# A two-layer kernel on one core: the last two expert tiles added by selection products, K and V weights split among the tiles, the barrier between the layers taken out

## The chip, the cores and the metric

The kernel runs on one core of a Trainium2 chip. The core has a matmul engine (PE, with its weight loads as PEld), a vector engine (DVE), an activation engine (ACT), a general engine (POOL) and a queue engine (SP, in the trace SPq) that issues most transfers. Each works through its own instructions in order and waits on semaphores for the others. The metric is the time of the kernel on the device in microseconds (us); lower is better.

## What is computed

Two layers on 2 x 512 tokens of 256 numbers, in fp32. The first layer runs a state-space scan beside a mixture of experts (each token goes to 2 of 8 experts), multiplies the two and adds the result to the tokens; the second does the same with attention and a sign-weight layer.

```python
x = L0_attn_x
xn = _layernorm(x, axis=-1)
s = _L0_attn_ref(xn, ...)              # projections, convolution, chunked scan, out projection
g = _silu(_L0_ffn_ref(xn, ...))        # top-2 of 8 experts, weighted sum of their outputs
x = x + s * g
xn = _layernorm(x, axis=-1)
s = _L1_attn_ref(xn, ...)              # 32 query heads, 8 key/value heads of 64
g = _silu(_L1_ffn_ref(xn, ...))
x = x + s * g
```

## The kernel before, in words

**Experts.** The 2 x 1024 (token, expert) pairs are sorted by expert into NJ = 23 tiles of 128 rows. For a tile j, POOL gathers the tokens' rows from memory (X on POOL), PE transposes them (X, turn_x), and multiplies with the expert's weights in three pieces (H1, H2, H3 in hidden); ACT takes the silu and DVE multiplies the halves to hE; PE projects back (P, project). DVE scales each row by its weight into y_row (rows, P on DVE), and POOL scatters the 128 rows to y_rows in memory, at the place given by to_row (P on POOL). The weights of a tile lie in one of three slots of wm; SP loads them as slots come free. X and P of PE share one PSUM bank: turn_x(j) waits for row_taken of tile j - 3.

**Scan.** The 1024 tokens are also cut into 8 chunks of 128. Chunk c has on PE the steps F (scan_decay: two fp32 matmuls of 512 columns), C (scan_front: a 128x128 product and four transposes), Y (scan_back) and O (out_rows). Between them ACT does exps (F) and scales (C), DVE the products (C, Y), y_lo (L) and the residual (O, which adds to semaphore s_part), POOL the mixes.

**Order.** The function side_by_side gives each step of tiles and chunks a place on one axis, 4 units for a tile, and each engine does its own steps in that order. CHUNK_AT says where each chunk begins. In the steps' names below the number is the tile or the chunk: P20 is the projection of tile 20, Y7 the scan_back of chunk 7.

**Between the layers.** After the last tile SP waits until all scatters have landed (row_out) and reads y_rows back as gy, two rows for each token. DVE adds the two (mixed_pair), ACT takes the silu, DVE multiplies with the scan's result s_tok and adds to x_tok (add_pair) and makes row statistics (pair_stats), for 4 pairs of token tiles. SP then loads the K and V weights of the second layer (kv_raw), ACT scales and rounds them to the upper part (kv_hi), POOL takes the rest (kv_lo). Then every engine calls end_phase, a barrier of all five. After it come the last statistics, the normalisation (xn1), its transposes (turn_norm), the K, Q and V products (make_k, make_q, make_v) and the attention proper.

```python
def end_phase(eng):
    k = ends[eng.engine] = ends.get(eng.engine, 0) + 1
    eng.drain().then_inc(phase_done, 1)
    eng.wait_ge(phase_done, 5 * k)
```

Of the kernel before, what the change touches and what calls it, by code (L numbers as in the profile page):

```python
# [152 lines left out]
K_MOVES = 4 * 16  # L153


def layered_kernel(nc, x, params, consts, select, rope, w_in, w_out, w_moe, w_moe_tail, w_qkv, w_o, w_sign, out):
# [4 lines left out]
    with ctx:  # L161
# [103 lines left out]
        w_out_sb = Map(weights_at)("w_out_sb", [P, NCH, C])  # L265
# [50 lines left out]
        assert back.at <= last.at
        kv_raw = last("kv_raw", [P, 2, KC, KVH * HD])
        kv_hi = last("kv_hi", [P, 2, KC, KVH * HD], F32R)
        kv_lo = last("kv_lo", [P, 2, KC, KVH * HD], F32R)
# [19 lines left out]
        q_mix = kv_raw[:, :, :, :]  # L339
# [12 lines left out]
        p_hi = kv_hi[:, :, :, :].rearrange("p a k n -> p (a k) n")  # L352
        p_lo = kv_lo[:, :, :, :].rearrange("p a k n -> p (a k) n")
# [24 lines left out]
        phase_done = sem("phase_done")  # L378
# [50 lines left out]
        ends = {}  # L429

        def end_phase(eng):

            k = ends[eng.engine] = ends.get(eng.engine, 0) + 1
            eng.drain().then_inc(phase_done, 1)
            eng.wait_ge(phase_done, 5 * k)

# [23 lines left out]
        def _(sp):  # L460
# [6 lines left out]
            sp.dma_start(w_out_sb[:, :, :], w_out).then_inc(w_out_in, 16)  # L467

# [166 lines left out]
        def _(dve):  # L635
# [47 lines left out]
            vec.memset(ssm[:, :, 0:TAPS - 1], 0.0).then_inc(ones_ready, 1)  # L683
            then(vec.memset(chosen[:, NT, :], 0.0))
# [213 lines left out]

            for engine, op, n in side_by_side():
# [31 lines left out]
            def mixed_pair(n):  # L931
                dve.wait_ge(pair_in[n], 32)
                ts = slice(2 * n, 2 * n + 2)
                TT(gate_y[:, ts, :], gy[:, 0, ts, :], gy[:, 1, ts, :], ALU.add).then_inc(mixed, 1)
# [150 lines left out]
        def _(act):  # L1085
# [39 lines left out]
            for n, (b, kind, m) in enumerate(PROJS):  # L1125
# [49 lines left out]
            for engine, op, n in side_by_side():  # L1175
# [39 lines left out]
            for n in range(NT // 2):
                act.wait_ge(mixed, n + 1)
                actv(gate_y[:, 2 * n:2 * n + 2, :], gate_y[:, 2 * n:2 * n + 2, :], ACT.Silu).then_inc(gated, 1)
            actv(sv[:, 8, :], sv[:, 0, :], ACT.Sqrt)
            act.wait_ge(kv_in, 96)
            actv(kv_raw[:, 0, :, 0:2 * P], kv_raw[:, 0, :, 0:2 * P], ACT.Copy, scale=HD ** -0.5).then_inc(k_scaled, 1)  # L1220
            actv(kv_hi[:, 1, :, :], kv_raw[:, 1, :, :], ACT.Copy)
            act.wait_ge(k_scaled, 1)
            actv(kv_hi[:, 0, :, 0:2 * P], kv_raw[:, 0, :, 0:2 * P], ACT.Copy).then_inc(w_hi_done, 1)
            end_phase(act)


# [121 lines left out]
        def _(gp_):  # L1348
# [53 lines left out]
            for engine, op, n in side_by_side():  # L1402
# [14 lines left out]
            gp_.wait_ge(w_hi_done, 3)  # L1417
            GT(kv_lo[:, 1, :, :], kv_raw[:, 1, :, :], kv_hi[:, 1, :, :].bitcast(F32), ALU.subtract)
            GT(kv_lo[:, 0, :, 0:2 * P], kv_raw[:, 0, :, 0:2 * P], kv_hi[:, 0, :, 0:2 * P].bitcast(F32), ALU.subtract).then_inc(w_lo_done, 1)
            end_phase(gp_)  # L1420


# [62 lines left out]
        def _(pe):  # L1485
# [231 lines left out]
            def make_k(r, b, k, bk):  # L1717
                w_h, w_l = (wk_hi, wk_lo) if r else (kv_hi[:, 0, :, :], kv_lo[:, 0, :, :])
                on_rows(bk[:, :], lambda c: w_h[:, c, k * P:(k + 1) * P], lambda c: w_l[:, c, k * P:(k + 1) * P], b).then_inc(kx_full, 1)

            def make_v(t):
# [3 lines left out]
                for c in range(KC):  # L1725
                    ins = split3(bank[t // TB * 2 + t % 2][:, :], xnT_hi[:, c, ts], xnT_lo[:, c, ts], kv_hi[:, 1, c, :], kv_lo[:, 1, c, :],
# [198 lines left out]
```

## Time and profile before

| what | value |
|---|---|
| time, median of 3 runs | 783.19 us (781.56 to 783.24) |
| the profiled execution | 780.78 us, of which the span of instructions is 779.0 us |
| busy in the span | PE 706.5 us (91%), DVE 477.7 (61%), ACT 417.9 (54%), POOL 399.3 (51%) |
| chain that ended last | PE 64%, DVE 10%, POOL 9%, ACT 8%, issue 6% |

The profile is of one execution, 2.4 us below the median of the three timed ones. A share of busy time is an average over stages with different limits, so it says little of one stage. "Issue" in the chain is time in which the engine waited for nothing that the profile shows, and PEclk or clock is the granted clock of PE as a part of full speed. PE's instructions in fp32 are recorded twice each (x16 are 8 matmuls).

### The profile page before, as it was taken

Reading aid. Unit: us, or ns where it says so; the run is one execution under the profiler, and the core shown is the slowest. Engines: PE = TensorE matmul, PEld = TensorE weight load, DVE = VectorE, ACT = ScalarE, POOL = GpSimd, SP = SyncE. Lnnn points to the kernel's source line nnn. Section 1 sums busy time; section 2 is a strip of 40 time slices with the busy share of each in tenths; the row PEclk is TensorE's granted clock in tenths of the full one; section 3 lists DMA queues with packets and bytes.
Section 4 is the critical chain, followed back from the end, with each engine's and each line's share of the span. In section 5 each row is a group of like instructions: output and inputs, shape, how many; then the busy total and the mean of one; then the engine's idle time right before and its main releaser. Section 6 shows DMA issues by size and latency. Waiting matters only on the chain.

```text
span 779.0 us, 13360 instructions
## 1 busy us (share of the span) xinstructions
PE 706.5 (91%) x4536; PEld 618.6 (79%) x4536; DVE 477.7 (61%) x1023; ACT 417.9 (54%) x1043; POOL 399.3 (51%) x451
## 2 busy tenths in 40 slices
PE   2999999999999991388889999999999999999995
PEld 2887989989989981266678888888888888888874
DVE  7582644423323445485566787777877778777764
ACT  4446244233233234236467776677766777667663
POOL 1412442332332220326777776787767877677460
PEclk9899999999999996599899999999999999999999
DMA  5075877778787505235224323322233222232001
GB/s 187 28 253 186 280 251 249 237 253 254 248 254 250 171 15 155 41 116 147 82 69 117 67 62 69 89 69 64 65 69 89 71 58 67 58 89 56 1 1 54
DMA packets 101859, 96.21 MB, mean 124 GB/s; under 512 B 50592, under 2 KB 72032, under 8 KB 101664
## 3 DMA queue, kind: packets, MB, share of 16 engines
q1 hardware_dynamic: 99584, 89.33, 39.6%
q0 software_dynamic: 2208, 6.03, 2.2%
q8 instruction: 36, 0.59, 0.3%
q14 instruction: 31, 0.25, 0.1%
HBM read 69.24 MB, written 9.31 MB: 101 GB/s over the span
## 4 chain that ended last, share of the span: by engine, by line
PE 64%; DVE 10%; POOL 9%; ACT 8%; issue 6%; SPq 1%; POOLq 1%; DMA 1%; DVEq 0%; ACTq 0%
PE bank L1631 15%; PE bank L1491 8%; PE bank L1665 8%; PE bank L1492 8%; PE bank L1493 8%; PE bank L1487 6%; POOL prob L1449 5%; ACT prob L1264 3%; PE bank L1752 3%; DVE nmax L1010 2%; PE bank L1753 2%; POOL q_lo L1461 2%; ACT kv_hi L1271 2%; DVE o_lo L1023 1%; POOL wq_lo L1429 1%
## 5 line engine op out<-in xcount | busy, mean ns | idle before, releaser
L1449 POOL TENSOR_TENSOR prob<-prob,rinv 128x128 f32<-128x128 f32 (+3 forms) x256 | 177.6, 724 | 102.1 <-DVE rinv L1015 102.1
L1264 ACT ACTIVATE prob<-bank,nmax 128x512 f32<-128x512 f32 (+3 forms) x256 | 133.2, 528 | 45.4 <-DVE nmax L1010 43.9
L1019 DVE TENSOR_TENSOR kv_lo<-bank,kv_hi 128x512 fp32r<-128x512 f32 x160 | 110.0, 687 | 52.7 <-ACT kv_hi L1271 51.8
L1271 ACT ACTIVATE kv_hi<-bank 128x512 fp32r<-128x512 f32 x160 | 96.3, 602 | 78.7 <-PE bank L1487 78.6
L1631 PEld LDWEIGHTS bank<-xgT,wm 128*128 128x128 f32 x920 | 108.1, 192 | 5.3 <-issue 3.8
L1631 PE MATMUL bank<-xgT,wm 128*128 128x128 f32 x920 | 110.3, 275 | 0.5 <-ACT xgT L1173 0.5
L1487 PE MATMUL bank<-cst,prob 128*128 128x128 f32 x640 | 97.8, 276 | 3.0 <-POOL prob L1449 1.2
L1010 DVE TENSOR_REDUCE nmax<-bank 128x1 f32<-128x512 f32 (+2 forms) x192 | 91.1, 502 | 10.8 <-PE bank L1755 10.2
L1491 PE MATMUL bank<-kv_hi,v_lo 128*128 128x128 f32 (+3 forms) x256 | 93.2, 364 | 0.3 <-DVE kv_lo L1019 0.3
L1752 PE MATMUL bank<-kT,qT 128*128 128x512 f32 (+3 forms) x256 | 81.6, 324 | 11.2 <-ACT prob L1264 7.2
L912 DVE TENSOR_TENSOR hE<-sil,bank 128x512 f32<-128x512 f32 x23 | 15.8, 688 | 111.0 <-PE bank L1631 80.5
L1493 PE MATMUL bank<-kv_hi,v_hi 128*128 128x128 f32 (+3 forms) x256 | 82.6, 323 | 0.0
L1492 PE MATMUL bank<-kv_lo,v_hi 128*128 128x128 f32 (+3 forms) x256 | 82.6, 322 | 0.0
L1415 POOL DMA_INDIRECT y_rows<-y_row,to_row x23 | 25.8, 1123 | 107.8 <-DVE y_row L885 107.8
L1487 PEld LDWEIGHTS bank<-cst,prob 128*128 128x128 f32 x640 | 73.6, 142 | 5.9 <-POOL prob L1449 3.3
L1753 PE MATMUL bank<-kT,qT 128*128 128x512 f32 (+3 forms) x256 | 74.4, 322 | 0.0
L1752 PEld LDWEIGHTS bank<-kT,qT 128*128 128x128 f32 x256 | 48.1, 188 | 20.9 <-issue 7.1
L1665 PE MATMUL bank<-wm,hE 128*128 128x256 f32 x230 | 53.5, 379 | 0.0
L1264 ACT ACTIVATION_READ_ACCUMULATOR prob<-bank,nmax 128x1 f32 x256 | 52.5, 205 | 0.0
L1753 PEld LDWEIGHTS bank<-kT,qT 128*128 128x128 f32 x256 | 48.3, 189 | 3.9
L1493 PEld LDWEIGHTS bank<-kv_hi,v_hi 128*128 128x128 f32 x256 | 48.6, 190 | 2.8
L1491 PEld LDWEIGHTS bank<-kv_hi,v_lo 128*128 128x128 f32 x256 | 48.7, 190 | 0.9 <-DVE kv_lo L1019 0.8
(301 smaller groups left out, 1479.0 us busy)
## 6 DMA issues: line engine op xcount, KB each, us to landing
wm<-in_w_moe SPq DMA_DIRECT2D x23, 1280.0 KB
wm<-in_w_moe SPq DMA_DIRECT2D x23, 640.0 KB, 5.7
qT<-q_hi SPq DMA_DIRECT2D x124, 64.0 KB, 2.0
qT<-q_lo SPq DMA_DIRECT2D x124, 64.0 KB, 2.0
k_exp<-k_rows SPq DMA_DIRECT2D x56, 64.0 KB, 2.0
wtl<-in_w_moe_tail SPq DMA_DIRECT2D x46, 64.0 KB
gy<-y_rows SPq DMA_DIRECT2D x8, 256.0 KB, 4.8
wq_raw<-in_w_qkv SPq DMA_DIRECT2D x32, 64.0 KB, 2.5
```

Source lines behind the costliest of these rows:

```text
L1019: TT(p_lo[:, b_, :], bank[2 + b_ % 2][:, :], p_hi[:, b_, :].bitcast(F32), ALU.subtract).then_inc(plo_done, 1)
L1264: ins = actv(prob[:, i % 2, h, POFF[j]:POFF[j] + (j + 1) * P], bk[:, at:at + (j + 1) * P], ACT.Exp, bias=nmax[:, i % 2, h, j:j + 1], accum ...
L1271: actv(p_hi[:, b_, :], bank[2 + b_ % 2][:, :], ACT.Copy).then_inc(phi_done, 1)
L1449: ins = GT(seg, seg, rinv[:, i % 2, k, j:j + 1].to_broadcast([P, (j + 1) * P]), ALU.mult)
L1487: return nc.tensor.transpose(dst, src, ident)
L1491: mm(dst, w_l, m_h, start=start, stop=False)
L1492: mm(dst, w_h, m_l, start=False, stop=False)
L1493: return mm(dst, w_h, m_h, start=False, stop=stop)
L1631: ins = mm(dst, w(c), xgT[:, u, c, :], start=c == 0, stop=c == KC - 1)
L1665: ins = mm(bank[3][:, 0:C], hE[:, u, i * P:(i + 1) * P], wm[:, s, i, PJ:WM] if i < FULL else ptl[:, s, :], start=i == 0, stop=i == HC - 1)
L1752: mm(dst, qs, kT[:, b, 0, 0:n], start=(h, j, at) == SCORES[k][0], stop=False)
L1753: mm(dst, qs, kT[:, b, 1, 0:n], start=False, stop=False)
```

## The change

**Tiles 21 and 22 are not scattered.** POOL has no P step for them (PICKED = 2). DVE makes for each a 128 x 8 x 128 matrix of zeros and ones (pick) that says which token each row belongs to. After the last tile PE makes for each of the 4 pairs of token tiles one sum in a PSUM bank (sum_pair): the two rows read back, each times the unit matrix, and the rows of y_row of both tiles times their selection matrices. ACT takes the silu from the bank. So that rows which no tile wrote are zero, SP fills the first 2048 rows of y_rows with zeros at the start (a memset of zeros by DVE, one transfer of 2 MB), and the first gather and the gates wait for it.

**Read-back.** SP reads back after the scatters of the first 21 tiles, once s_part is 4, into the first halves of xs and gate, which the scan has then done with.

**K and V weights.** SP loads them when row_full is 21, into the slot that tile 20 has left; ACT's rounding is the step "kv" of side_by_side at 4 * NJ - 4.6, POOL's the step at 4 * NJ - 3.7. q_mix, p_hi and p_lo get places of their own.

**Order.** CHUNK_AT goes in steps of 11.5 instead of 12.

**Barrier.** end_phase is gone from all engines; single waits stand in its place (SP for s_part = 8, POOL for row_full = 23, PE for turns_ready and w_lo_done). The transposes of the rotation tables (turns) lie between the second and third sum, and ACT's Sqrt table load ahead of the last wait.

```diff
         if j > 0:
-            z += [(at + 3.1, "PE", "P", j - 1), (at + 3.2, "DVE", "P", j - 1), (at + 3.3, "POOL", "P", j - 1)]
+            z += [(at + 3.1, "PE", "P", j - 1), (at + 3.2, "DVE", "P", j - 1)]
+        if 0 < j <= NJ - PICKED:
+            z += [(at + 3.3, "POOL", "P", j - 1)]
...
+    z += [(4 * NJ - 4.6, "ACT", "kv", 0), (4 * NJ - 3.7, "POOL", "kv", 0)] + [(42.6 + 6 * i, "DVE", "pick", i) for i in range(PICKED)]
...
-CHUNK_AT = [3 + 12 * c for c in range(NT)]
+PICKED = 2
+CHUNK_AT = [3 + 11.5 * c for c in range(NT)]
...
+            sp.wait_ge(ones_ready, 3)
+            sp.dma_start(y_rows[0:2 * T, :].rearrange("(a p) c -> p a c", p=P),
+                         zeros.unsqueeze(1).to_broadcast([P, 2 * T // P, C])).then_inc(xn_out, 16)
...
-            sp.wait_ge(row_full, NJ)
+            sp.wait_ge(row_full, NJ - 2)
+            for c in range(KC):
+                for h in range(2):
+                    load_wk(0, c, h, wk0[:, c, h * P:(h + 1) * P])
+                sp.dma_start(wv0[:, c, :].rearrange("p (g d) -> p g d", d=HD),
+                             w_qkv[:, :, c, (GQ + 1) * HD:(GQ + 2) * HD].rearrange("g p d -> p g d")).then_inc(kv_in, 16)
             yv = y_rows[0:2 * T, :].rearrange("(k t p) c -> p k t c", k=2, p=P)
             for u in range(2):
-                sp.wait_ge(row_out[u], (NJ + 1 - u) // 2 * 16)
+                sp.wait_ge(row_out[u], (NJ - PICKED + 1 - u) // 2 * 16)
+            sp.wait_ge(s_part, TB)
             for n in range(NT // 2):
                 for k in range(2):
-                    sp.dma_start(gy[:, k, 2 * n:2 * n + 2, :], yv[:, k, 2 * n:2 * n + 2, :]).then_inc(pair_in[n], 16)
...
-            end_phase(sp)
+                    sp.dma_start(gy(k, n).rearrange("p (t c) -> p t c", c=C), yv[:, k, 2 * n:2 * n + 2, :]).then_inc(pair_in[n], 16)
+            sp.wait_ge(s_part, NT)
...
+            def pick(i):
+
+                j = NJ - PICKED + i
+                then(TS(spare_f[:, 0:NT], edges[:, 0:NT], -1.0, tab[:, 1, j:j + 1], ALU.mult, ALU.add))
+                TT(picks[:, i, :, :], lane_no.unsqueeze(1).to_broadcast([P, NT, P]),
+                   spare_f[:, 0:NT].unsqueeze(2).to_broadcast([P, NT, P]), ALU.is_equal).then_inc(table_ready, 1)
...
+                elif op == "kv":
+                    act.wait_ge(kv_in, 96)
+                    actv(wk0[:, :, :], wk0[:, :, :], ACT.Copy, scale=HD ** -0.5).then_inc(k_scaled, 1)
+                    actv(wv0_hi[:, :, :], wv0[:, :, :], ACT.Copy)
+                    act.wait_ge(k_scaled, 1)
+                    actv(wk0_hi[:, :, :], wk0[:, :, :], ACT.Copy).then_inc(w_hi_done, 1)
...
+            def sum_pair(n):
+
+                dst = bank[MIXED_IN[n]]
+                pe.wait_ge(pair_in[n], 32)
+                for k in range(2):
+                    mm(dst[:, :], ident, gy(k, n), start=k == 0, stop=False)
+                for i in range(PICKED):
+                    j = NJ - PICKED + i
+                    pe.wait_ge(table_ready, 5 + i)
+                    pe.wait_ge(row_taken, j + 1)
+                    for t in range(2):
+                        ins = mm(dst[:, t * C:(t + 1) * C], picks[:, i, 2 * n + t, :], y_row[:, j % 2, :],
+                                 start=False, stop=i == PICKED - 1 and t == 1)
+                ins.then_inc(mixed, 1)
+
+            pe.wait_ge(s_part, NT)
+            sum_pair(0)
+            sum_pair(1)
             pe.wait_ge(rp4_ready, 3)
```

ACT, before, from the silu of H1 of tile 22 (sil of 128x512) to the first work after the tiles; dx are the scales of chunk 7, y_hi is ahead of O7:

```order
L1192 ACTIVATE sil<-bank 128x512
L1165 ACTIVATE dx<-xs,par 128x128 x4
L1197 ACTIVATE sil<-bank 128x128
L1198 ACTIVATE sil<-bank 64x128
L1145 ACTIVATE y_hi<-gate 128x512
L1211 ACTIVATE turns<-bank 128x512 x3
```

ACT, after, from the second half of tile 21's silu on; wk_118 is wk0 and wv_hi is wv0_hi:

```order
L1213 ACTIVATE sil<-bank 128x128
L1214 ACTIVATE sil<-bank 64x128
L1200 ACTIVATE wk_118<-wk_118 128x512
L1201 ACTIVATE wv_hi<-wv_119 128x1024
L1203 ACTIVATE wk_hi<-wk_118 128x512
L1208 ACTIVATE sil<-bank 128x512
L1213 ACTIVATE sil<-bank 128x128
L1214 ACTIVATE sil<-bank 64x128
L1155 ACTIVATE y_hi<-gate 128x512
L1227 ACTIVATE xs<-bank 128x512 x2
```

The three roundings of the K and V weights now stand between the silus of tile 21 and those of tile 22, and y_hi of chunk 7 behind both.

PE, before, from P20 (wm,hE and ptl,hE) to P21; xgT,wm x8 and x12 are H1 and parts of H2 and H3 of tile 22, decay_in is F7, CT,BT and xs are C7:

```order
L1665 MATMUL bank<-wm,hE 128x256 x5
L1665 MATMUL bank<-ptl,hE 128x256
L1572 MATMUL bank<-decay_in,cst 128x512
L1573 MATMUL bank<-decay_in,ones 128x512
L1631 MATMUL bank<-xgT,wm 128x128 x8
L1580 MATMUL bank<-CT,BT 128x128
L1487 MATMUL bank<-cst,xs 128x128 x4
L1631 MATMUL bank<-xgT,wm 128x128 x12
L1631 MATMUL bank<-xgT,wtl 128x128 x2
L1665 MATMUL bank<-wm,hE 128x256 x5
L1665 MATMUL bank<-ptl,hE 128x256
L1597 MATMUL bank<-mix,x_dt 128x128
```

PE, after, from F7 to the H1 and H2 of tile 22 that stand together behind P20; cst,xg is X of tile 22:

```order
L1581 MATMUL bank<-decay_in,cst 128x512
L1582 MATMUL bank<-decay_in,ones 128x512
L1496 MATMUL bank<-cst,xg 128x128 x2
L1640 MATMUL bank<-xgT,wm 128x128 x8
L1589 MATMUL bank<-CT,BT 128x128
L1496 MATMUL bank<-cst,xs 128x128 x4
L1640 MATMUL bank<-xgT,wm 128x128 x4
L1640 MATMUL bank<-xgT,wtl 128x128 x2
L1674 MATMUL bank<-wm,hE 128x256 x5
L1674 MATMUL bank<-ptl,hE 128x256
L1640 MATMUL bank<-xgT,wm 128x128 x16
```

F7 and C7 have moved ahead of P20, into tile 21.

DVE, before, around chunk 6's front (cbm to x_end); the y_row rows are those of tiles 17 and 18:

```order
L885 TENSOR_SCALAR y_row<-bank,tab 128x256
L912 TENSOR_TENSOR hE<-sil,bank 128x512
L843 TENSOR_TENSOR cbm<-bank,cst 128x128
L848 TENSOR_TENSOR w_end<-dts,within 128x4
L851 TENSOR_TENSOR x_dt<-bank,dts 128x512
L852 TENSOR_TENSOR x_end<-bank,w_end 128x512
L915 TENSOR_TENSOR hE<-sil,bank 128x128
L916 TENSOR_TENSOR hE<-sil,bank 64x128
L885 TENSOR_SCALAR y_row<-bank,tab 128x256
```

DVE, after, the same place; the y_row rows are those of tiles 16 and 17:

```order
L897 TENSOR_SCALAR y_row<-bank,tab 128x256
L931 TENSOR_TENSOR hE<-sil,bank 128x512
L934 TENSOR_TENSOR hE<-sil,bank 128x128
L935 TENSOR_TENSOR hE<-sil,bank 64x128
L855 TENSOR_TENSOR cbm<-bank,cst 128x128
L860 TENSOR_TENSOR w_end<-dts,within 128x4
L863 TENSOR_TENSOR x_dt<-bank,dts 128x512
L864 TENSOR_TENSOR x_end<-bank,w_end 128x512
L897 TENSOR_SCALAR y_row<-bank,tab 128x256
```

The rows of tile 17 (the second y_row) now stand behind the front of chunk 6, where before the front stood behind them.

## Rows read from the trace of the kernel before

**Rows 1.** Stages: length, busy us (count) by engine, clock, DMA share, GB/s.
```profile
100.00:284.00 184.00, 184.00 (x1330) 168.53 (x1329) 68.15 (x148) 65.18 (x138) 57.85 (x53) 1.00 0.72 230
...
293.00:324.00 31.00, 3.44 (x29) 3.23 (x30) 15.21 (x42) 8.89 (x15) 6.64 (x7) 0.60 0.47 117
```

**Rows 2.** Waits from 284 to 330 us: total, times, longest, in us.
```profile
PE bank L1487 <- DVE xn L963: 27.1, 2, 26.9
```

**Rows 3.** The chain of work: start, us, engine and line.
```profile
274.64 2.59 PE bank L1665 x12
277.23 0.86 PE bank L1572 x2
...
278.95 1.78 PE bank L1631 x16
...
311.54 7.45 POOLq L434
```

**Rows 4.** Timeline, DVE after the barrier: start, us, operation, [idle before].
```profile
319.02 0.75 DVE L946 BATCH_NORM_STATS2 stats<-x_tok 128x6 f32<-128x256 f32 x2 [7.57 <-POOLq L434]
```

**Rows 5.** Timeline, last tiles, PE, ACT and DVE.
```profile
277.07 1.02 PE L1572 MATMUL bank<-decay_in,cst 128*128 128x512 f32 x2
...
280.09 1.28 ACT L1192 ACT_TABLE_LOAD   x1
...
280.57 0.39 PE L1580 MATMUL bank<-CT,BT 128*128 128x128 f32 x2
...
281.23 2.84 PE L1631 MATMUL bank<-xgT,wm 128*128 128x128 f32 x24
...
281.88 1.26 ACT L1165 ACTIVATE dx<-xs,par 128x128 f32<-128x128 f32 x4
...
287.06 0.46 PE L1597 MATMUL bank<-mix,x_dt 128*128 128x128 f32 x2
...
289.78 2.32 PE L1665 MATMUL bank<-wm,hE 128*128 128x256 f32 x10
...
292.97 0.68 DVE L873 TENSOR_TENSOR y_lo<-gate,y_hi 128x512 fp32r<-128x512 f32 x1
...
293.70 0.38 PE L1491 MATMUL bank<-w_out_hi,y_lo 128*128 128x256 f32 x1 [1.18 <-DVE y_lo L873]
...
295.18 1.47 PE L1487 MATMUL bank<-cst,turns 128*128 128x128 f32 x12
```

**Rows 6.** Timeline, the K and V loads (SPq issues) and ACT's rounding.
```profile
299.99 4.01 SPq L471 DMA_DIRECT2D kv_raw<-in_w_qkv  x4
...
304.04 1.63 SPq L526 DMA_DIRECT2D kv_raw<-in_w_qkv  x2
...
309.40 0.63 ACT L1220 ACTIVATE kv_raw<-kv_raw 128x512 f32<-128x512 f32 x1 [0.40 <-DMA kv_raw<-in_w_qkv]
...
310.89 0.61 ACT L1223 ACTIVATE kv_hi<-kv_raw 128x512 fp32r<-128x512 f32 x1
...
321.62 2.08 SPq L471 DMA_DIRECT2D wk_raw<-in_w_qkv  x4
```

**Rows 7.** Loads of kv_raw.
```profile
DMA to landing us min/median/max: 4.0/4.5/5.3
```

**Rows 8.** Loads of wq_raw at 319 us.
```profile
DMA to landing us min/median/max: 2.0/2.3/2.9
```

**Rows 9.** Timeline, PE after its wait at 340 us.
```profile
342.62 0.50 PE L1491 MATMUL bank<-xnT_hi,kv_lo 128*128 128x512 f32 x1 [2.37 <-DVE xnT_lo L972]
```

**Rows 10.** Windows of 2 us, columns as in rows 1.
```profile
328.00:330.00 2.00, 2.00 (x6) 1.61 (x6) 0.00 (x0) 1.87 (x3) 0.00 (x0) 0.50 0.03 8
...
344.00:346.00 2.00, 2.00 (x6) 1.61 (x5) 1.87 (x3) 0.00 (x0) 0.00 (x0) 0.50 0.11 28
346.00:348.00 2.00, 2.00 (x7) 1.56 (x6) 0.83 (x2) 0.00 (x0) 0.00 (x0) 0.69 0.41 103
```

**Rows 11.** Timeline, DVE, the 128x2048 comparison.
```profile
43.08 2.29 DVE L794 TENSOR_TENSOR lanes<-in_lane,count_f 128x2048 f32<-128x2048 f32 x1
```

More of the change, by code:

```diff
@@ L153 @@
 K_MOVES = 4 * 16
+MIXED_IN = (5, 6, 7, 3)
 def layered_kernel(nc, x, params, consts, select, rope, w_in, w_out, w_moe, w_moe_tail, w_qkv, w_o, w_sign, out):
@@ L264, in layered_kernel @@
         assert first.at <= weights_at
-        w_out_sb = Map(weights_at)("w_out_sb", [P, NCH, C])
+        w_out_sb = Map(top_at - NCH * C * 4)("w_out_sb", [P, NCH, C])
+        picks = Map(hT_at + 2 * KC * T * 4)("picks", [P, PICKED, NT, P])
+        zeros = gate[:, 0, 0:C]
         table = Map(both.at)
@@ L308, in layered_kernel, with gy, gate_y @@
         weights = Map(weights_at)
-        wm = weights("wm", [P, 3, FULL, WM])
         wtl = weights("wtl", [P, 3, KC, P])
         ptl = weights("ptl", [P, 3, C])
-        back = Map(weights_at)
-        gy = back("gy", [P, 2, NT, C])
-        gate_y = back("gate_y", [P, NT, C])
+        wm = weights("wm", [P, 3, FULL, WM])
+        def gy(k, n):
+            return (xs, gate)[k][:, n, 0:HALF]
+        def gate_y(n):
+            return xs[:, n, 0:HALF].rearrange("p (t c) -> p t c", c=C)
+        kv_at = weights.at - FULL * WM * 4
+        assert (NJ - 3) % 3 == 2
+        raw, lower, upper = Map(kv_at), Map(kv_at), Map(kv_at + 3 * KC * HALF * 2)
+        wk0, wv0 = raw("wk0", [P, KC, 2 * P]), raw("wv0", [P, KC, KVH * HD])
+        wk0_lo, wv0_lo = lower("wk0_lo", [P, KC, 2 * P], F32R), lower("wv0_lo", [P, KC, KVH * HD], F32R)
+        wk0_hi, wv0_hi = upper("wk0_hi", [P, KC, 2 * P], F32R), upper("wv0_hi", [P, KC, KVH * HD], F32R)
+        assert raw.at <= kv_at + 3 * KC * HALF * 2 and upper.at <= top_at
         last = Map(top_at - 3 * 2 * KC * KVH * HD * 4)
[L316 to L319, printed above, removed]
+        q_mix = last("q_mix", [P, 2, 2, HALF])
+        p_hi = last("p_hi", [P, 4, HALF], F32R)
+        p_lo = last("p_lo", [P, 4, HALF], F32R)
+        assert kv_at >= last.at - 2 * 4 * HALF * 4
         attn = Map(low)
@@ L427, in layered_kernel @@
         ohi_done, olo_done, wo_full = sems("ohi_done olo_done wo_full")
[L429 to L435, printed above, removed]
         def stepper(eng, signal):
@@ L921, in _ @@
                     centre_signs()
+                elif op == "pick":
+                    pick(n)
                 elif op == "C":
@@ L929, in _ @@
                     residual(n)
[L931 to L934, printed above, removed]
             def add_pair(n):
-                xt2, g2 = x_tok[:, 2 * n:2 * n + 2, :], gate_y[:, 2 * n:2 * n + 2, :]
+                xt2 = x_tok[:, 2 * n:2 * n + 2, :]
                 dve.wait_ge(gated, n + 1)
-                dve.wait_ge(s_part, 2 * n + 2)
-                then(TT(g2, g2, s_tok[:, 2 * n:2 * n + 2, :], ALU.mult))
-                TT(xt2, xt2, g2, ALU.add).then_inc(x_ready, 1)
+                dve.wait_ge(s_part, NT)
+                then(TT(gate_y(n), gate_y(n), s_tok[:, 2 * n:2 * n + 2, :], ALU.mult))
+                TT(xt2, xt2, gate_y(n), ALU.add).then_inc(x_ready, 1)
             def pair_stats(n):
@@ L1208, in _ @@
                     upper_y(n)
-            act.wait_ge(turns_full, 1)
-            for i in range(3):
-                ins = actv(turns[:, i, :], bank[i][:, :], ACT.Copy)
+            for n in range(NT // 2):
+                act.wait_ge(mixed, n + 1)
+                actv(gate_y(n), bank[MIXED_IN[n]][:, :].rearrange("p (t c) -> p t c", c=C), ACT.Silu).then_inc(gated, 1)
+                if n == 1:
+                    act.wait_ge(turns_full, 1)
+                if n > 0:
+                    ins = actv(turns[:, n - 1, :], bank[n - 1][:, :], ACT.Copy)
             ins.then_inc(turns_ready, 1)
+            actv(sv[:, 8, :], ones[:, 0:NT], ACT.Sqrt)
             act.wait_ge(turns_full, 2)
             actv(wsT[:, :, :], bank[4][:, :].rearrange("p (k o) -> p k o", k=KC), ACT.Copy).then_inc(turns_ready, 1)
[L1215 to L1224, printed above, removed]
             def split_wq(g):
@@ L1410, in _ @@
                     mixes(n)
+                elif op == "kv":
+                    gp_.wait_ge(w_hi_done, 3)
+                    GT(wv0_lo[:, :, :], wv0[:, :, :], wv0_hi[:, :, :].bitcast(F32), ALU.subtract)
+                    GT(wk0_lo[:, :, :], wk0[:, :, :], wk0_hi[:, :, :].bitcast(F32), ALU.subtract).then_inc(w_lo_done, 1)
                 elif op == "X":
@@ L1416, in _ @@
                                             in_=y_row[:, n % 2, :], in_offset=None).then_inc(row_out[n % 2], 16)
[L1417 to L1420, printed above, removed]
+            gp_.wait_ge(row_full, NJ)
             for v in (v_hi, v_lo):
@@ L1691, in _ @@
             ins.then_inc(turns_full, 1)
+            sum_pair(2)
+            sum_pair(3)
             pe.wait_ge(wsign_ready, KC)
@@ L1725, in make_v @@
                 for c in range(KC):
-                    ins = split3(bank[t // TB * 2 + t % 2][:, :], xnT_hi[:, c, ts], xnT_lo[:, c, ts], kv_hi[:, 1, c, :], kv_lo[:, 1, c, :],
+                    ins = split3(bank[t // TB * 2 + t % 2][:, :], xnT_hi[:, c, ts], xnT_lo[:, c, ts], wv0_hi[:, c, :], wv0_lo[:, c, :],
                                  c == 0, c == KC - 1)
@@ L1811, in attend @@
                         ins.then_inc(sign_full, 1)
+            pe.wait_ge(turns_ready, 1)
             for k in range(KC * BATCH):
@@ L1815, in _ @@
             pe.wait_ge(lo_done, KC * BATCH + 2)
+            pe.wait_ge(w_lo_done, 4)
+            pe.wait_ge(turns_ready, 2)
             for k in range(2):
```

23 lines of the change are left out of this document (4 added, 19 removed).

## The prediction

> **What bounds the kernel now.** The table of stages is read first: from 100 to 284 us PE is busy for all of 184.00 us, and from 293 to 324 us for only 3.44 of 31.00 us, at a granted clock of 0.60 [rows 1]. Time can come only from that hole. The waits say what PE waits for there: 26.9 us for xn, the normalised tokens of the second layer [rows 2]. The chain of work says what comes late: after the last scatter POOL stands for a long "issue", until ACT has rounded the K and V weights; it splits them, and then 7.45 us go at the barrier, on POOL's queue, before DVE goes on [rows 3]. Meanwhile the scatter lands, is read back, summed and added, which DVE has finished but for two row statistics at 311.45. It starts these two at 319.02 [rows 4]. All that follows them is unchanged by the edit, but for the clock; so the question is when they start.
>
> **Part 1, what is moved ahead of P20.** F, C, Y, O are the four PE steps of a chunk, H1, H2, H3, X, P those of a tile. T is the moment when PE goes on after P20, the projection of tile 20: 277.07 before [rows 5]. CHUNK_AT goes in steps of 11.5 for 12, so F7 and C7 now stand before P20. F7 is two pairs of 0.86 [rows 3]; C7 lasts from 280.57 to 281.23 [rows 5]. That is 1.72 + 0.66 = 2.4 us which now pass before T; the work is the same.
> The chunks also meet the tiles in other places. At most of them I find slack left. At chunk 6 I do not: PE has P17, H1 of tile 19, then the transposes X of tile 20, which share bank 3 with P17 and wait until DVE has taken P17's rows. Counted from the end of H1 of tile 18, ACT waits for X19 (2.3), loads the Exp table (1.28), does two exps (1.2), four skips (1.26), loads the Silu table (1.28) and does two silus (0.6): done at 8.0 [rows 5]. DVE then multiplies (0.6), does the front of chunk 6 (1.6) and the rows (0.5): 10.7. PE wants to go on at 1.72 + 0.20 + 1.78 + 0.66 + 1.35 + 2.59 + 1.78 = 10.1 [rows 3, 5]. A stall of **0.6 us**; bounds 0 and 1.5 for all chunks together. T becomes 277.07 + 2.4 + 0.6 = **280.1**.
>
> **Part 2, the K and V weights.** SP issues their six loads once row_full is 21, which is P20's end, so they cannot start before T. ACT has its "kv" step before the silu of tile 22's H1, and ACT works in order, so that silu waits for all six loads. Issue: four K loads at 2.08/4 = 0.52 each when the queue is free (321.62), two V loads at 1.63/2 = 0.82, together 3.7 us; the last begins at T + 0.2 + 2.9 = T + 3.1 [rows 6]. Landing: before, these loads took 4.0 to 5.3 us, behind 2 MB of read-back [rows 7]; the same shape with a free queue took 2.0 to 2.9 [rows 8]. The queue is free here, but a V load is four times as large: 3.0. ACT starts at T + 6.2 and needs 2.1 (309.40 to 310.89, and 0.61) [rows 6]: T + 8.3; then the silu, 0.6: T + 8.9.
> The Trainium skill, page "DMA: Bandwidth & Descriptors", section "Anatomy of one DMA", gives a DMA a fixed 2.0 us and its bytes at 436 GB/s: 2.6 us for 256 KB, where I take 3.0 from the rows. By it the gain would be 0.4 us more; the rows here, with their short pieces, are all that show this shape.
> Behind that silu stand on DVE hE (0.7), the four operations of Y7 (2.7, y_ready at T + 12.3), tile 22's other products (0.6), P21's rows (0.5), then y_lo; and PE starts O7 0.73 after y_lo starts (292.97 to 293.70) [rows 5]: **T + 14.0**. PE itself has H1 and H2 (1.78 each), Y7 (287.06 to 289.78, 2.72), H3 (1.35) and P21 (2.59), and is free at T + 10.2 [rows 3, 5]. It stands **3.8 us** idle, where before it waited 1.18.
> The split on POOL ends long before PE needs it, 40 us after T, and only memsets stand behind it; if it were late, the make_k products would be. With it the barrier goes: 319.02 - 311.45 = 7.6 us, the real saving [rows 4].
>
> **Part 3, the clock.** At 342.62 PE had been idle for 2.37 us [rows 9]; the granted clock then fell from 1.00 to 0.50, that is from 2.4 to 1.2 GHz, and was back before 348 (0.50 from 344 to 346, 0.69 from 346 to 348, of which I read a low stretch of 3.4 us) [rows 10]. A wait of 3.8 us will do this too. Such a stretch costs half of itself, 1.7, less what still falls into the wait: I take **1.6**. Bounds: 0 if the level holds, 3 if the stretch is as long as after 324, where it was still low at 330 [rows 10].
>
> **Part 4, selection products for read-back.** After O7 (1.48: 293.70 to 295.18) and P22 (2.59) PE reaches A = 280.1 + 14.0 + 4.1 + 1.6 = **299.8**; before, P22 ended at 292.4 (289.78 + 2.59) [rows 3, 5]. No row shows a selection product; its shape is in the rows. Each sum_pair is two fp32 products of 512 columns (0.86 each, as one of F's) and four of 256 columns (2.59/6 = 0.43 each, as in a projection): 3.45 [rows 3]. Four are 13.8, the 12 transposes among them 1.4 (the x12 row at 295.18): the last ends at A + 15.2 [rows 5]. Silu 0.6, two DVE operations 1.3, the statistics of pair 2 0.7, 0.1 of handover: A + 17.9 = **317.7**. Before, this way took 311.45 - 292.4 = 19.0 us. So the products alone save 1.1 us, and fill 13.8 us of PE that stood idle.
> The read-back is hidden: its eight loads go out behind K/V at about T + 5, are issued in 4 us, as before (the K loads followed them at 299.99), and A is 10 us later; landing after A they would cost what they are late [rows 6].
> Costs at nothing: the two masks on DVE, each half of "lanes" (2.29) [rows 11], lie among tiles 10 to 12, where DVE is busy 68.15 of 184.00 us [rows 1]; without that cover each is 1.2. The zero fill of 2 MB goes out behind w_out at the start, and its users, the gates and the first scatter, come more than 20 us later; the cover is the projection stage.
>
> **The sum.** 319.02 - 317.7 = 1.3 us gained. Before, the low clock lasted some 6 us after PE's restart at 324 and fell again at 344; both depend on where the waits fall, and for the two together I take 0.6 us back, between 0 and 3. Gain **1.9 us**: the profiled execution would go from 780.78 (span 779.0) to 778.9. It lies 2.4 below the median of the runs, 783.19, and against that I forecast **781.3**. What a measurement of this kernel can tell from no change is about 0.2%, 1.6 us.
>
> **The rivals.**
> - The K/V stall is short. If the last load lands 1.9 us after it is issued, near the quickest of [rows 8], the idle is 2.7 us and the clock may hold: 1.1 + 1.6 more, a gain of 4.6: 778.6. For no stall at all (1.9 + 3.8 + 1.6 = 7.3, 775.9) ACT would need the data at T + 2.4, before the last load is issued. Chance 0.2 for a gain over 3.8.
> - It ends slower, by the K/V loads alone. Before, 9.4 us passed from the first issue (299.99) to ACT's start (309.40) [rows 6]; I have 6.0. If they take as long here, because P20's scatter and the first read-back loads share the engines with them, O7 comes 3.4 us later, PE is idle for 7.2 us, and the low stretch is nearer to that after 324 (1.4 more): 3.4 + 1.4 - 1.9 = 2.9 lost, 786.1. It decides when they land about 1.9 us later than I have it, and turns slower by 0.2% at 3. Against it: they were behind 2 MB then, and here they are first. Chance 0.2, with stalls among the tiles that I have not seen.
> - What is won is given back: the stall and the product path eat the barrier's 7.6 us up to 1.6 on either side. Chance 0.3; my bare sum, 1.3, lies in it: 782.
> - The change does not empty the hole, because another engine holds the old order (POOL's step after P20, SP's wait for s_part before the wq loads): the time would stay at 783. I see nothing that waits there, and give it no chance of its own.
>
> **How the numbers follow.** The forecast (gain 1.6 to 3.8) has 0.3, the short stall 0.2, no change 0.3, slower 0.2. So faster is 0.5, same 0.3, slower 0.2. The forecast's own range is 779.4 to 781.6. To hold 8 in 10 the range goes 1 us beyond the short stall's 778.6, and to 0.5 short of the slow case's 786.1: 777.6 to 785.6.
>
> **What the changed profile would show.** ACT idle for 6 to 8 us until the K/V loads land at T + 6.2; PE idle for some 4 us before O7, released by y_lo. A low clock in O7 and P22. Four groups of sums of 3.45 us, the last ending 15 us after P22. DVE's last statistics near 317.7. PE's hole before xn about 7 us for 26.9. No wait on the read-back. A stall of 0.6 us before the transposes of tile 20, and PE otherwise full from 100 us on. I am wrong if the K/V data come at T + 4 or T + 9, if the clock holds through the wait before O7, or if several chunks stall.

## The result: slower by 0.57%

| | median | runs | against before (95% interval) |
|---|---|---|---|
| before | 780.01 us (777.10 to 783.24) | 16 | |
| this kernel | 784.58 us (783.43 to 786.75) | 16 | 1.0057 (1.0043 to 1.0072) |

4.6 us are lost at the medians where 1.9 were to be gained. The median of the kernel before is 3.2 us below that of its first three runs. The profiled execution took 783.43 us (span 781.6), 2.65 more than that of before. I read the stages first, as in [rows 1]:

```profile
100.00:284.00 184.00, 182.36 (x1313) 166.89 (x1312) 74.81 (x154) 62.05 (x135) 60.06 (x55) 1.00 0.73 227
...
293.00:324.00 31.00, 21.64 (x88) 16.15 (x88) 14.87 (x39) 7.29 (x13) 4.00 (x6) 0.85 0.19 39
```

The hole is filled as meant, 21.64 us busy for 3.44, but the tiles have lost 1.6 us of PE. The waits of 284 to 350 us (total, times, longest) show 7.7 us where [rows 2] had 26.9, a new wait of ACT, and 5.5 us for y_lo where [rows 5] had 1.18:

```profile
ACT wk L1200 <- DMA wv<-in_w_qkv: 8.9, 1, 8.9
...
PE bank L1496 <- DVE xn L972: 7.7, 1, 7.7
...
PE bank L1500 <- DVE y_lo L885: 5.5, 1, 5.5
```

The timeline of the changed kernel, all engines, answers to [rows 4 to 6]. The first row is H1 of tile 0, which in the trace of before stands at 66.37:

```profile
64.81 2.05 PE L1640 MATMUL bank<-xgT,wm 128*128 128x128 f32 x16 [0.47 <-ACT xgT L1183]
...
166.64 0.46 PE L1606 MATMUL bank<-mix,x_dt 128*128 128x128 f32 x2 [0.73 <-POOL c_dec L1409]
...
252.99 0.41 PE L1496 MATMUL bank<-cst,xg 128*128 128x128 f32 x2 [0.52 <-issue]
...
281.14 3.73 PE L1640 MATMUL bank<-xgT,wm 128*128 128x128 f32 x32
...
284.19 0.52 SPq L531 DMA_DIRECT2D wv<-in_w_qkv  x1
...
288.19 0.63 ACT L1200 ACTIVATE wk<-wk 128x512 f32<-128x512 f32 x1 [8.86 <-DMA wv<-in_w_qkv]
...
290.19 0.58 ACT L1208 ACTIVATE sil<-bank 128x512 f32<-128x512 f32 x1
290.37 2.34 POOL L1423 TENSOR_TENSOR wv_lo<-wv,wv_hi 128x1024 fp32r<-128x1024 f32 x1 [7.26 <-ACT wk_hi L1203]
...
291.41 1.85 DVE L872 TENSOR_TENSOR state<-state,since 128x512 f32<-128x512 f32 x1
292.68 1.71 POOL L1424 TENSOR_TENSOR wk_lo<-wk,wk_hi 128x512 fp32r<-128x512 f32 x1
293.30 0.69 DVE L875 TENSOR_TENSOR state<-state,bank 128x512 f32<-128x512 f32 x1
...
296.98 0.58 PE L1500 MATMUL bank<-w_out_hi,y_lo 128*128 128x256 f32 x1 [5.53 <-DVE y_lo L885]
...
302.93 1.02 PE L1701 MATMUL bank<-xs,cst 128*128 128x512 f32 x2
...
318.02 0.60 PE L1496 MATMUL bank<-cst,wsg 128*128 128x128 f32 x4
...
320.19 1.40 DVE L962 BATCH_NORM_STATS2 stats<-x_tok 128x6 f32<-128x256 f32 x4
...
323.31 1.26 POOL L1438 TENSOR_TENSOR wq_lo<-wq_raw,wq_hi 128x512 fp32r<-128x512 f32 x1 [18.23 <-ACT wq_hi L1241]
323.38 1.22 DVE L679 TENSOR_SCALAR sv<-sv 128x8 f32<-128x8 f32 x1
...
326.36 3.64 PE L1496 MATMUL bank<-cst,xn 128*128 128x128 f32 x16 [7.74 <-DVE xn L972]
```

Tile 0 starts 1.56 us earlier than before, but that is no merit of the change: over the eleven traces of both kernels and the experiments it starts either at 64.7 to 64.9 or at 66.3 to 66.8, kernels with the changed code on either side. The start goes with the granted clock of the projection stage: in the 16 us from 16 on it was 0.89 to 0.91 in the six traces that start early, this one among them, and 0.82 to 0.85 in the five late ones, the kernel before among them. So I compare places in the program by their distance from that row. **D** is the distance from tile 0's H1 to the start of xn's transposes, where PE's hole ends: 323.95 - 66.37 = **257.6** before, 326.36 - 64.81 = **261.55** after. That is 4.0 lost, where the prediction (1.3 gained, without the clock) has D at 256.3: a miss of 5.3 us.

| step | predicted | measured | miss |
|---|---|---|---|
| T, against before, from tile 0 | +3.0 | 216.33 - 210.70 = +5.6 | 2.6 |
| T to O7's start | 14.0 | 296.98 - 281.14 = 15.8 | 1.8 |
| O7 and P22, with the clock | 4.1 + 1.6 | 302.93 - 296.98 = 5.95 | 0.25 |
| A to the last statistics | 17.9 | 320.89 - 302.93 = 18.0 | 0.1 |
| last statistics to PE's start | 4.9 as before | 326.36 - 320.89 = 5.5 | 0.5 |

(320.89 is the second half of the row at 320.19.) The five make up the 5.3. The theory to test: the loss is made by three things, stalls among the tiles from the steps of 11.5, ACT's wait for the K/V loads, and DVE and POOL holding each other up. The rival: the new sums or the lost barrier are themselves the cost, or a stall taken away comes back elsewhere.

### The profile page after: what moved, and what is told of

Same layout as the page of the kernel before. It is cut to its first block, busy times and chain, and to the rows that moved or that the text cites. A ratio compares the mean times of both kernels' runs of the same rounds, so it can differ in the third digit from the quotient of the medians.

```text
span 781.6 us, 13464 instructions
## 1 busy us (share of the span) xinstructions
PE 722.8 (92%) x4583; PEld 629.8 (81%) x4584; DVE 482.5 (62%) x1024; ACT 417.2 (53%) x1043; POOL 397.4 (51%) x449
## 4 chain that ended last, share of the span: by engine, by line
PE 63%; DVE 11%; POOL 9%; ACT 7%; issue 4%; SPq 2%; DMA 2%; DVEq 0%; ACTq 0%; POOLq 0%
PE bank L1640 13%; PE bank L1500 8%; PE bank L1674 7%; PE bank L1501 7%; PE bank L1496 7%; PE bank L1502 7%; POOL prob L1458 5%; ACT prob L1274 3%; PE bank L1779 3%; DVE nmax L1019 2%; PE bank L1780 2%; POOL q_lo L1470 2%; ACT p_hi L1281 2%; DVE o_lo L1032 1%; POOL wq_lo L1438 1%
## 5 line engine op out<-in xcount | busy, mean ns | idle before, releaser
L1028 DVE TENSOR_TENSOR p_lo<-bank,p_hi 128x512 fp32r<-128x512 f32 x160 | 110.0, 688 | 52.3 <-ACT p_hi L1281 51.4
L1281 ACT ACTIVATE p_hi<-bank 128x512 fp32r<-128x512 f32 x160 | 96.3, 602 | 78.0 <-PE bank L1496 78.0
L1500 PE MATMUL bank<-p_hi,v_lo 128*128 128x128 f32 (+3 forms) x256 | 93.2, 364 | 0.3 <-DVE p_lo L1028 0.3
L1429 POOL DMA_INDIRECT y_rows<-y_row,to_row x21 | 22.7, 1082 | 118.3 <-DVE y_row L897 92.6
L1502 PE MATMUL bank<-p_hi,v_hi 128*128 128x128 f32 (+3 forms) x256 | 82.5, 322 | 0.0
L1501 PE MATMUL bank<-p_lo,v_hi 128*128 128x128 f32 (+3 forms) x256 | 82.5, 322 | 0.0
L931 DVE TENSOR_TENSOR hE<-sil,bank 128x512 f32<-128x512 f32 x23 | 15.8, 687 | 63.4 <-PE bank L1640 37.4
L1208 ACT ACTIVATE sil<-bank 128x512 f32<-128x512 f32 x23 | 13.7, 596 | 72.2 <-PE bank L1640 45.5
L1502 PEld LDWEIGHTS bank<-p_hi,v_hi 128*128 128x128 f32 x256 | 48.7, 190 | 2.7
## 6 DMA issues: line engine op xcount, KB each, us to landing
y_rows<-gate SPq DMA_DIRECT2D x1, 2048.0 KB, 13.9
```

The source lines that it names most:

```text
L1028: TT(p_lo[:, b_, :], bank[2 + b_ % 2][:, :], p_hi[:, b_, :].bitcast(F32), ALU.subtract).then_inc(plo_done, 1)
L1281: actv(p_hi[:, b_, :], bank[2 + b_ % 2][:, :], ACT.Copy).then_inc(phi_done, 1)
L1500: mm(dst, w_l, m_h, start=start, stop=False)
L1501: mm(dst, w_h, m_l, start=False, stop=False)
L1502: return mm(dst, w_h, m_h, start=False, stop=stop)
```

## The experiments

Each has 4 to 12 timed runs and one trace. Each was compared with runs of the kernel before on its own chip, whose medians were 779.8 (the first four rows), 780.2 and (last one) 781.2 us, so the ratios are to be compared. The differences below are of medians; by the ratios they come out up to 1 us otherwise (picked1 against kv_late_step12: 3.8 by medians, 4.8 by ratios). D is of the traced execution alone.

| kernel | median | against before (95%) | D |
|---|---|---|---|
| kv_late | 778.28 | 0.9981 (0.9967 to 0.9995) | 255.3 |
| pool_late | 782.68 | 1.0041 (1.0026 to 1.0056) | 261.55 |
| kv_late_step12 | 775.71 | 0.9951 (0.9937 to 0.9966) | 253.1 |
| before_step115 | 786.46 | 1.0093 (1.0072 to 1.0114) | 263.6 |
| barrier | 776.01 | 0.9953 (0.9936 to 0.9969) | 253.0 |
| wq_held | 774.94 | 0.9935 (0.9918 to 0.9953) | 252.0 |
| picked1 | 771.94 | 0.9890 (0.9874 to 0.9906) | 249.6 |
| all_in | 769.46 | 0.9855 (0.9833 to 0.9877) | 246.2 |
| all_in_held | 771.80 | 0.9884 (0.9867 to 0.9901) | 249.3 |

**kv_late.**

```diff
-    z += [(4 * NJ - 4.6, "ACT", "kv", 0), ...
+    z += [(4 * NJ - 1.05, "ACT", "kv", 0), ...
             sp.wait_ge(s_part, NT)
+            sp.wait_ge(k_scaled, 1)
```

> The changed kernel with ACT's rounding of the K and V weights moved from ahead of tile 22's silus to behind y_hi of chunk 7 (SP waits for it before it loads the next K weights). Theory (the 8.9 us in which ACT stands for the K/V loads is the loss): O7 starts about 11 us after P20's end in place of 15.8, so PE's wait of 5.5 us shrinks to about 1, and O7 and P22 run at full clock (4.1 us for 5.95); 4.6 + 1.8 = 6.4 us gained, about 778. Rival (the loss lies among the tiles, and the stall at the end only changes its place, because the rounding now delays the first sum's silu): gain under 1.5 us, 783 or more.

Measured: 6.3 us less than the changed kernel, and the kernel is now faster than before, by 0.2%. Its timeline:

```profile
283.05 3.73 PE L1641 MATMUL bank<-xgT,wm 128*128 128x128 f32 x32
...
288.61 0.69 DVE L873 TENSOR_TENSOR state<-state,since 128x512 f32<-128x512 f32 x1 [1.04 <-PE bank L1609]
...
294.54 0.39 PE L1501 MATMUL bank<-w_out_hi,y_lo 128*128 128x256 f32 x1 [1.18 <-DVE y_lo L886]
...
298.65 1.02 PE L1702 MATMUL bank<-xs,cst 128*128 128x512 f32 x2
...
322.07 3.65 PE L1497 MATMUL bank<-cst,xn 128*128 128x128 f32 x16 [7.73 <-DVE xn L973]
```

O7 starts 11.5 us after T (283.05) for 15.8, and O7 with P22 takes 4.1 for 5.95. The sum, 6.2, is the change of D, within 0.1. Nothing comes back later. The gain is not of ACT's wait alone: POOL's split now begins later as well, and DVE's state operation takes 0.69 us instead of 1.85. One step of the order decided the sign of the whole change.

**pool_late.**

```diff
                     gp_.wait_ge(w_hi_done, 3)
+                    gp_.wait_ge(row_full, NJ)
                     GT(wv0_lo[:, :, :], wv0[:, :, :], wv0_hi[:, :, :].bitcast(F32), ALU.subtract)
```

> The changed kernel with POOL's split of the K and V weights held back until P22 has ended. Theory (DVE and POOL slow each other when both work on large tiles): DVE's state operation of chunk 7 takes 0.7 us in place of 1.85, the next starts directly behind it, O7 comes 1.2 to 1.7 us earlier; 1.2 to 2.3 us gained with the clock, about 783. Rival (the state operation was long for another reason, or the wait moves elsewhere): it stays at 1.85, time 784.6 within 0.5.

Its timeline, and two windows of 2 us (columns as in [rows 1]):

```profile
291.69 0.68 DVE L872 TENSOR_TENSOR state<-state,since 128x512 f32<-128x512 f32 x1
...
296.09 0.58 PE L1501 MATMUL bank<-w_out_hi,y_lo 128*128 128x256 f32 x1 [4.61 <-DVE y_lo L885]
...
303.03 1.02 PE L1702 MATMUL bank<-xs,cst 128*128 128x512 f32 x2
```

```profile
300.00:302.00 2.00, 2.00 (x6) 1.55 (x5) 0.00 (x0) 0.00 (x0) 0.00 (x0) 0.50 0.46 72
302.00:304.00 2.00, 2.00 (x9) 1.38 (x8) 0.48 (x1) 0.00 (x0) 0.65 (x1) 0.97 0.89 203
```

The mechanism is shown: the operation takes 0.68 for 1.85, and O7 starts 14.9 us after T (281.17) for 15.8. Its worth is not settled. In this execution the clock stayed at 0.50, that is 1.2 GHz, through the window 300 to 302, where the changed kernel already had 0.75:

```profile
300.00:302.00 2.00, 2.00 (x8) 1.63 (x8) 0.37 (x1) 0.00 (x0) 0.00 (x0) 0.75 0.21 33
```

So O7 and P22 took 6.9 us for 5.95 and D did not move. Over the runs the median fell by 1.9, but the intervals of the two ratios overlap. The traced execution is 2.15 us faster than that of the changed kernel, with the same D: the difference lies behind D, where the granted clock was higher, 1.00 from 346 to 356 for 0.86.

**kv_late_step12.**

```diff
-CHUNK_AT = [3 + 11.5 * c for c in range(NT)]
+CHUNK_AT = [3 + 12 * c for c in range(NT)]
-    z += [(4 * NJ - 1.05, "ACT", "kv", 0), (4 * NJ - 3.7, "POOL", "kv", 0)] ...
+    z += [(4 * NJ + 2.6, "ACT", "kv", 0), (4 * NJ + 3.5, "POOL", "kv", 0)] ...
```

> As kv_late, but with the chunks in steps of 12 again (the rounding then behind y_hi once more, POOL's split behind the last tile). Theory (steps of 11.5 cost 3.2 us of small stalls among the tiles, and F7 and C7 ahead of P20 buy nothing once the K/V wait is gone): P20 ends 5.6 us earlier by the same start, P22 and O7 end 2.8 us earlier; about 3 us less than kv_late, 775. Rival (steps of 11.5 pay for their stalls, since y_lo comes early and PE never waits for it): the same as kv_late or slower, 778 or more.

Measured: 2.6 us less than kv_late, D 2.2 less. From tile 0's H1 (64.66) to P20's end (275.35) it is 210.69 us, as before (210.70), and the two stalls that the changed kernel shows at 166.64 and 252.99 are gone. The steps of 11.5 did not pay: kv_late still waits 1.18 for y_lo, just as before.

**before_step115.** The kernel before with the second line of that diff reversed.

> The kernel before with CHUNK_AT in steps of 11.5 and nothing else changed. Theory (3.2 us of stalls, and O7's 1.5 us now stand ahead of P22, whose scatter starts the read-back): 4.7 us slower, about 784.7. Rival (the stalls belong to other parts of the change, such as the masks or the zero fill): only the 1.5 us of O7, about 781.5, or no change at all.

Measured: slower by 6.6 us at the medians, D 6.0. From tile 0 (66.29) to P20's end (282.55) it is 216.26, and in the changed kernel 216.33: all of the stalls belong to the steps of 11.5, none to masks or zero fill. My 4.7 was short by the wait for y_lo, which did not go away but moved ahead of P22:

```profile
294.04 0.39 PE L1491 MATMUL bank<-w_out_hi,y_lo 128*128 128x256 f32 x1 [1.18 <-DVE y_lo L873]
```

**barrier.** end_phase is put back in all five engines.

```diff
             sp.wait_ge(k_scaled, 1)
+            end_phase(sp)
...
+            end_phase(dve)
             pair_stats(NT // 2 - 1)
```

> kv_late_step12 with the barrier of all five engines put back at the same places as in the kernel before (DVE ahead of its last statistics, SP ahead of the wq loads). Theory (what the barrier cost before was that it waited for the late K/V loads, rounding and split; with these done early it costs little): DVE passes it when ACT's last copy is done, about 1.5 us late, 777.2. Rival (the barrier is a cost of its own): some 7 us, 783.

Measured: the same as kv_late_step12 in time and D. The wait that was 7.57 us in [rows 4] is here

```profile
312.86 0.75 DVE L973 BATCH_NORM_STATS2 stats<-x_tok 128x6 f32<-128x256 f32 x2 [0.45 <-ACTq L450]
```

These 0.45 us are won back because the wq loads come later with the barrier, so that POOL's split misses the small operation of the next experiment (it takes 0.17). A barrier costs what its last comer is late. In the kernel before that was POOL, and only half of its lateness was work:

```profile
313.88 1.26 POOL L1419 TENSOR_TENSOR kv_lo<-kv_raw,kv_hi 128x512 fp32r<-128x512 f32 x1
```

DVE was ready at 311.45 and POOL's split ended at 315.14, but the drain with which POOL enters the barrier ended only at 318.99, 3.9 us later ([rows 3], 311.54 and 7.45). In this run POOL's drain ends 3.7 us after its split as well (300.5 and 296.8), but that is 12 us before DVE comes, and it costs nothing. Spans on POOL are rough, but the two traces agree.

**wq_held.**

```diff
                 gp_.wait_ge(wqhi_done, g + 1)
+                if isinstance(g, int) and g == 0:
+                    gp_.wait_ge(xn_ready, NT + 2 * TB)
```

> kv_late_step12 with POOL's split of the first wq held back until DVE has made all of xn. Theory (DVE and POOL slow each other): the small DVE operation that takes 1.22 us beside POOL's split takes 0.17 again, xn comes 1.05 us earlier, 774.7. Rival (that row is long for another reason, or wq_lo then comes too late for the Q products): 775.7 or more.

Measured: D falls by 1.05, as forecast; the median falls by 0.8, to a ratio whose interval overlaps the other's. First the rows of kv_late_step12, then those of wq_held:

```profile
314.67 1.26 POOL L1439 TENSOR_TENSOR wq_lo<-wq_raw,wq_hi 128x512 fp32r<-128x512 f32 x1 [16.16 <-ACT wq_hi L1242]
314.74 1.22 DVE L680 TENSOR_SCALAR sv<-sv 128x8 f32<-128x8 f32 x1
```

```profile
316.42 0.17 DVE L680 TENSOR_SCALAR sv<-sv 128x8 f32<-128x8 f32 x1
...
319.64 1.27 POOL L1441 TENSOR_TENSOR wq_lo<-wq_raw,wq_hi 128x512 fp32r<-128x512 f32 x1 [19.46 <-DVE xn L973]
```

An operation on 8 columns takes seven times as long, because POOL's had begun 0.07 us before it.

**picked1.** PICKED = 1: tile 21 is scattered and read back, tile 22 alone comes in by products.

> kv_late_step12 with one tile (22) added by selection products and tile 21 scattered and read back. Theory (the sums are bound by PE, 3.45 us each): each sum loses two products of 256 columns, 2.59 for 3.45, so four end 3.4 us earlier, about 772.3. Rival (the scatter of tile 21 and the read-back behind it land after P22 and O7 have ended): PE waits for the first sums by 3 us or more, 775 or slower.

Measured: 3.8 us less than kv_late_step12, D 3.5 less. PE waits 0.56 us before its first sum, as in kv_late_step12, so the scatter and the read-back are still hidden. One tile more by products cost PE 0.86 us for each sum and hid nothing.

**all_in.** Both of the last two, and:

```diff
+            for n in range(NT // 2):
+                dve.wait_ge(pair_in[n], 32)
+                TT(gy(0, n), gy(0, n), gy(1, n), ALU.add).then_inc(summed, 1)
...
-                pe.wait_ge(pair_in[n], 32)
-                for k in range(2):
-                    mm(dst[:, :], ident, gy(k, n), start=k == 0, stop=False)
+                pe.wait_ge(summed, n + 1)
+                mm(dst[:, :], ident, gy(0, n), start=True, stop=False)
```

The transposes of the rotation tables come behind sum_pair(3), and ACT's copies of them behind its Sqrt table load.

> picked1 and wq_held together, and DVE adds the two read-back rows ahead of the sums, so that each sum has one product with the unit matrix (1.73 us for 2.59), and the transposes of the rotation tables come behind the fourth sum. Theory (all of this lies on PE's path from P22 to the last statistics): 3.4 more from the sums, 1.3 from the transposes, 1.0 from the split, 0.7 given back because ACT's copies then stand ahead of the square root: about 767. Rival (the read-back sets the start of the sums): PE waits for the rows, 770 or more.

Measured: 1.45% faster than the kernel before, the best of all, but 2.5 us short of the forecast:

```profile
294.83 2.35 POOL L1427 TENSOR_TENSOR wv_lo<-wv,wv_hi 128x1024 fp32r<-128x1024 f32 x1 [5.87 <-ACT wk_hi L1208]
...
295.80 4.80 DVE L968 TENSOR_TENSOR xs<-xs,gate 128x512 f32<-128x512 f32 x4
...
297.88 1.10 PE L1706 MATMUL bank<-xs,cst 128*128 128x512 f32 x2 [2.45 <-DVE xs L968]
```

DVE's four additions take 4.8 us for some 2.8, since POOL's split runs beside them, and PE waits 2.45 us for the first. After that DVE is the bound, with 2.0 us for each pair against PE's 1.73.

**all_in_held.** POOL's split of K and V waits for the four additions (gp_.wait_ge(summed, 4)).

> all_in with POOL's split of the K and V weights held back until DVE has added the four read-back pairs. Theory (DVE's additions took 1.2 us each because the split ran beside them): they take 0.7 each, PE waits 1.2 us less for the first sum, and about 1.2 us are gained, 768.3. Rival (the split then falls on the multiplications and additions to the tokens, on which the path lies now): nothing gained or up to 1 us lost, 769.5 to 770.5.

Measured: 2.3 us slower than all_in, D 3.0 longer; the rival holds, and by more than I gave it. The additions take 0.69 each and PE waits 1.21, but the last of them still ends no earlier, because three of the four now wait 0.8 us each for the rows read back, and the split then meets an addition and a multiplication on the path, which take 2.0 and 1.1 us more than in all_in:

```profile
299.42 2.66 POOL L1428 TENSOR_TENSOR wv_lo<-wv,wv_hi 128x1024 fp32r<-128x1024 f32 x1 [12.07 <-DVE xs L968]
...
299.90 2.73 DVE L959 TENSOR_TENSOR x_tok<-x_tok,xs 128x512 f32<-128x512 f32 x1
...
302.55 1.76 DVE L958 TENSOR_TENSOR xs<-xs,sT 128x512 f32<-128x512 f32 x1
```

The zero fill was not taken out by itself. Its transfer landed after 13.9 us, and from DVE's first statistics at 4.74 (4.72 before) to the first transposed tokens on ACT at 14.66 (14.64) the rows stand where they stood. With it in place kv_late_step12 takes no longer than before from tile 0 to P20's end.

## Why the prediction was wrong, step by step

Two terms of the sum were too small, and they turn the gain into a loss: the stalls among the tiles (part 1, 2.6 us) and the way from P20's end to O7 (part 2, 1.8 us). The range, 777.6 to 785.6, does contain the measured 784.58, but by luck: it was set against 783.19, and the kernel before has 780.01 over all its runs.

- **Part 1, "A stall of 0.6 us; bounds 0 and 1.5"** failed, by 2.6 us. The stall that I worked out is there, in size and place (0.52, before X of tile 20, at 252.99). But I looked closely at one chunk and took the others to have slack. From tile 0 to T the changed kernel takes 5.6 us more, of which the moved F7 and C7 are 2.4; 3.2 are stalls. Counted from one matmul's start to the next, 0.9 lies at Y of a chunk, where PE waits for POOL's c_dec, 0.7 at X of tile 20 (both with the waits shown above), and the rest mostly in six pieces of 0.2 to 0.3 that the waits don't list; the kernel before has none of them. before_step115 has the same 216.3 us. "I am wrong if several chunks stall" was the right warning, without a price in the sum.
- **Part 2, the K and V weights.** The mechanism was right: SP issues at T + 0.2, the last issue begins at T + 3.05, ACT works in order, and the silu waits. The size was off by 1.8. The last load took 3.98 us to land where I had 3.0, so ACT starts at T + 7.05 and not 6.2 (3.1 + 3.0 is 6.1, a slip of 0.1). The 2.6 us that the prediction works out beside it from the Trainium skill (page "DMA: Bandwidth & Descriptors", section "Anatomy of one DMA") were further off; that section is about transfers issued by POOL, and these are issued by SP. And the terms for DVE came from rows in which POOL was quiet. I followed POOL's split only to its own deadline ("ends long before PE needs it") and did not ask which engine it slows: the state operation took 1.85 us for 0.69.
- **Part 3, the clock: 1.6.** The clock fell as forecast, and O7 and P22 took 1.85 over full speed. The 0.6 us for the low clock behind xn held: from xn to PE's restart behind its wait for xnT_lo it is 344.40 - 326.36 = 18.0 us, before 342.62 - 323.95 = 18.7. One pair of executions can't tell this from luck, as the clock behind D in pool_late shows.
- **Part 4, the products.** Right in each term: 3.45 a sum, A + 18.0 to the last statistics. The read-back was hidden. The one thing missed is again POOL beside DVE: 1.05 us on the small operation at 323.38. Of these 0.5 remain against before, where another small operation, at 320.48, took 0.56 for 0.17 beside POOL's memset.
- **The barrier, "the real saving"**, was only one way to it. With K and V early the barrier costs nothing (barrier), and for that the change paid with a stall on the path where ACT was idle a few us later (kv_late). No run takes the barrier out with K and V as late as before. By the rows of before that would have been enough: POOL's split ended at 315.14, and PE read kv_lo for the first time at 327.81. This is argued, not shown.
- **The rivals.** The slower one had the right direction, but called for loads 3 us late. They were 0.85 late to ACT, and the stalls among the tiles and POOL beside DVE did the rest. I gave 0.2 to that side, "with stalls among the tiles that I have not seen".

What stays open: by D and the rows to 344 us the loss is 3.3 to 4.0, by the profiled times, 2.65 with the 1.56 us at the start, 4.2. Up to 0.9 us lie in the attention stage, and I have not traced them. What each part of the 3.2 us of stalls waits for was not told apart either; before_step115 shows that they belong to the steps of 11.5, not by which engine.

## What to carry to other kernels

When an order is shifted as a whole, a stall worked out at one place is a sample, not a bound: follow every chunk, or price the ones not followed. A step that waits for a transfer belongs behind all the work on its engine that someone waits for, and not at the first moment at which the data might be there; here 3.5 places on the axis were worth 6 us. And when work moves to another engine, ask not only whether it is done in time, but what runs beside it.

## What was not expected of the hardware

- **DVE and POOL hold each other up for whole operations.** The changed kernel's state operation starts at 291.41 and ends at 293.26, 0.55 us after POOL's split ends at 292.71; POOL's next split takes 1.71 us instead of 1.26. In all_in_held an addition of 0.69 us took 2.73, and one of 8 columns took 1.22 for 0.17 in kv_late_step12. The Trainium skill, page "SBUF — State Buffer", section "SBUF: two separate sides", says this: the two share a port pair as an exclusive lock, and who starts first has it for the whole instruction. It says so of DVE's operations in a 2-port mode or with both inputs in SBUF. These traces agree, in the exception too: at 293.30 an operation with one input in PSUM took its usual 0.69 us while POOL was at work. What they add is how it looks: no wait and no releaser, only a row that is longer than its form.
- **The same wait of PE leaves the clock low for different times.** Behind the wait for xnT_lo, 2.37 us in all three traces, the clock fell to 0.50 before and in the changed kernel, and stayed at 1.00 in pool_late. And after idle times of 5.5 and 4.6 us (changed kernel, pool_late), O7 and P22 took 5.95 and 6.9 us, for 4.1 at full clock: the shorter wait had the longer stretch at 1.2 GHz. A term for it needs a range of about 1 us.
- **The start differs by 1.5 us from trace to trace**, and goes with the clock in the projection stage, not with the kernel. Two profiles can be compared only from a common place on.
